# One decoder layer on one core: the same steps in another order of the turn, with tables of their own for the first and the last 900 steps

## The reference

```python
KV = x @ V;  V = 0.25 * V @ (13*I - KV @ (15*I - KV @ (7*I - KV)))      # pinv, 6 times, 64x64, 16 heads
out = attn1 @ (pinv(attn2) @ (attn3 @ v));  x = x + out @ Wout + bout   # 64 landmarks = means of 8 tokens
x = x + (softmax(mask(Q @ K.T / 4)) @ V) @ Wo.T + bo                    # cross-attention to 64 tokens
sel = argmax(softmax(gelu(x_n[last] @ Wp1 + bp1) @ Wp2 + bp2))          # one expert of 8 for each batch
x = x + 0.3 * ((gelu(x_n @ W1[sel] + b1[sel]) @ W2[sel] + b2[sel]) @ Wo_f + bo_f)
```

## Time and profile before

| what | us |
|---|---|
| median of 3 runs | 1443.07 (1442.46 to 1445.51) |
| span of the profiled execution | 1444.1 |
| TensorE busy in it | 1406.6 (97%) |
| VectorE / ScalarE / GpSimd busy | 1028.2 / 666.8 / 569.6 |

### The profile page before, as it was taken

The page is one execution under the profiler, slowest core; times in us unless marked ns, Lnnn a source line. Parts: engine busy times, 40 slices in busy tenths (PEclk is TensorE's granted clock), DMA queues, the critical chain, the costliest instruction groups (busy, mean ns, idle before and its releaser), DMA issues.

```text
span 1444.1 us, 54637 instructions
## 1 busy us (share of the span) xinstructions
PE 1406.6 (97%) x24180; PEld 927.0 (64%) x24180; DVE 1028.2 (71%) x2162; ACT 666.8 (46%) x1202; POOL 569.6 (39%) x799
## 2 busy tenths in 40 slices
...
DMA packets 40540, 53.25 MB, mean 37 GB/s; under 512 B 9698, under 2 KB 30450, under 8 KB 40306
## 3 DMA queue, kind: packets, MB, share of 16 engines
...
...
## 4 chain that ended last, share of the span: by engine, by line
PE 92%; DVE 5%; issue 2%; POOL 1%; ACT 0%; DVEq 0%; POOLq 0%; ACTq 0%
PE bank L1226 44%; PE bank L1244 8%; PE bank L1476 7%; PE bank L1254 6%; PE bank L1463 5%; PE bank L1431 2%; PE bank L1372 2%; PE bank L1325 2%; PE bank L1304 2%; PE bank L1234 2%; PE bank L1444 2%; PE bank L1361 2%; PE bank L1339 1%; PE bank L1465 1%; PE bank L1422 1%
## 5 line engine op out<-in xcount | busy, mean ns | idle before, releaser
L686 POOL TENSOR_TENSOR b<-ut,eye 128x256 f32<-128x256 f32 x192 | 136.4, 730 | 349.7 <-DVE ut L1066 320.2
L1096 DVE TENSOR_REDUCE m<-bank 128x8 f32<-128x512 f32 x128 | 82.3, 682 | 69.3 <-PE bank L1431 69.3
L1226 PE MATMUL bank<-xnT_a,wqkv 128*128 128x512 f32 x256 | 123.9, 607 | 0.0
L1226 PE MATMUL bank<-xnT_c,w1e 128*128 128x512 f32 x256 | 119.8, 604 | 0.0
L1226 PE MATMUL bank<-w2e,hT 128*128 128x256 f32 x512 | 117.9, 384 | 0.9 <-ACT hT L911 0.9
L1122 DVE RECIPROCAL oT_x<-bank 128x256 f32<-128x256 f32 x64 | 107.5, 1723 | 15.1 <-PE bank L1476 15.0
L1122 DVE RECIPROCAL oT<-bank 128x256 f32<-128x256 f32 x64 | 111.9, 1750 | 3.3 <-PE bank L1476 3.3
L1226 PEld LDWEIGHTS bank<-w2e,hT 128*128 128x128 f32 x512 | 94.9, 190 | 16.1 <-issue 1.7
L845 ACT ACTIVATE az<-bank 128x320 f32<-128x320 f32 x192 | 69.3, 401 | 76.2 <-PE bank L1244 73.6
L864 ACT ACTIVATE pT_x<-bank,neg_bias 128x512 f32<-128x512 f32 x128 | 78.0, 689 | 51.2 <-PE bank L1465 51.2
L1057 DVE SCALAR_TENSOR_TENSOR wb<-bank,eye 128x256 f32<-128x256 f32 x192 | 72.9, 413 | 34.7 <-PE bank L1244 34.6
...
## 6 DMA issues: line engine op xcount, KB each, us to landing
x_in<-in_x SPq DMA_DIRECT2D x16, 512.0 KB, 3.6
w1e<-in_W SPq DMA_DIRECT2D x16, 512.0 KB, 3.6
w2e<-w2o SPq DMA_DIRECT2D x16, 512.0 KB, 3.6
...
hT<-in_W2T SPq DMA_DIRECT2D x2, 512.0 KB, 5.7
...
w2o<-hT SPq DMA_DIRECT2D x2, 512.0 KB
```

The lines of the kernel that those rows point to most:

```text
L686: return g.tensor_tensor(b7[:, q, :], ut[:, q, :], eye[28 if it else 7][:].unsqueeze(1) .broadcast_to([P, 4, LM]), ALU.subtract).then_inc( ...
L1096: return v.tensor_reduce(m[x][:, :, j, 2 * k:2 * k + 2], tile(i, ("s" + x, k), j)[:].rearrange("p (t h c) -> p t h c", t=T, h=2), AX.X, AL ...
L1226: last = mm(dst, lhsT, rhs, start=(k == 0), stop=(k == len(pairs) - 1))
```

## The change

`TURN` is written anew: the same steps, at most 3 batches back instead of 6, in another order on every engine. A new table `FIRST` names the first 900 steps with their batch, as `LAST` does the last 900 (999 before). The setup steps stand in `FIRST` alone, so `once()` goes. The whole is 4411 steps before and after, 1307 of them on TensorE: before, 1011 came from the turns and 296 from `LAST`; now 264 from `FIRST`, 775 from the turns and 268 from `LAST`. `plan()`, `body()` and every instruction are as they were; lines after the tables lie 72 lower.

```diff
 TURN = """
-    S.fc D.mxx.1.3-5 D.mxx.0.1-5 D.mxx.0.3-5 P.y3.0-6 P.f.3-3 P.xnTa.0-3 A.xnTa.0-3 D.mxx.0.2-5
...
+    A.a.1-2 P.vx-3 D.recx.0.1-3 A.a.0-2 A.zT.1-2 D.recx.1.0-3 D.recx.1.1-3 P.z-2 G.b7.0.0-2 D.z-2 P.s1.1-2
...
+FIRST = """
+    S.x@0 S.w2.0@0 D.lnA@0 S.fc@0 G.lnA@0 P.f.0@0 S.w2.7@0 P.f.7@0 S.w2.6@0 D.nmA@0 P.f.6@0 P.xnTa.0@0
...
+    P.wx.0@15 A.nmC.1@15 P.y3.0@14 P.xnTc.1@15 D.wx.0@15 A.xnTc.1@15 P.gate@15 D.lnC.0@15 G.rsC.0@15
+    A.gate@15 P.logit@15 A.nmC.0@15 P.xnTc.0@15 A.xnTc.0@15 P.y3.1@14 D.logit@15 S.ew1@15 P.h.0@15 P.h.1@15
...
-def once(step):
-
-    return step[0] in ("fc", "w2", "f", "fb", "cn", "nmA", "cst", "kx")
...
 def program():
 
-    steps, last = [], set(LAST_STEPS)
+    steps, apart = [], set(FIRST_STEPS) | set(LAST_STEPS)
     for turn in range(BATCH + DEPTH):
         for engine, step, back in TURN_STEPS:
             i = turn - back
-            if 0 <= i < BATCH and not (i and once(step)):
-                if (engine, i, step) not in last:
-                    steps.append((engine, i, step))
-    return steps + LAST_STEPS
+            if 0 <= i < BATCH and (engine, i, step) not in apart:
+                steps.append((engine, i, step))
+    return FIRST_STEPS + steps + LAST_STEPS
```

More of the change, by code:

```diff
@@ new lines @@
+    D.rec1.0.1@15 D.o1.1@15 P.o1.0@15 P.xnTc.1@14 D.o1.0@15 P.w1.1@15 S.ctx@15 P.w1.0@15 D.w1.1@15
+    A.xnTc.1@14 G.rsC.0@14 D.lnB.1@15 D.w1.0@15 A.nmC.0@14 G.rsB@15 P.gate@14 D.lnB.0@15 G.lnB.0@15
+    P.y3.0@13 G.row@13 A.gate@14 A.nmB@15 P.xnTb.1@15 P.logit@14 A.xnTb.1@15 P.xnTb.0@15 P.xnTc.0@14
+    A.xnTb.0@15 P.qx.1@15 P.qx.0@15 A.qx.1@15 D.y3.0@13 P.sx.1@15 A.xnTc.0@14 A.qx.0@15 D.logit@14
+    D.mxx.1.0@15 D.mxx.1.3@15 P.sx.0@15 D.mxx.0.2@15 D.mxx.1.1@15 D.mxx.0.1@15 D.mxx.0.3@15 D.mxx.0.0@15
```

354 lines of the change are left out of this document (208 added, 146 removed).

## The result

The changed kernel takes 1447.87 us (median of 20 runs, 1441.85 to 1454.84), the kernel before 1443.64 (20 runs, 1440.89 to 1448.61). The ratio is 1.0029, 95% interval 1.0018 to 1.0040: slower, by little. The forecast was 1431, range 1417 to 1444. The profiled execution took 1447.92 with a span of 1446.1, 2.0 over the span of before. The new kernel's runs took 1.6 to 1.9 us more than their spans. Later runs of before took 1.8 to 2.1 over theirs, so its profiled execution (span 1444.1) took 1446 or little less, about 2 above its median. (Of the three runs that the prediction had, only 1445.51 is above that span; the text ahead of the prediction set the span beside the median and called it 1.0 above.) The new profile stands at its own median: the traces show half of the 4.2 us between the medians.

A forecast was written before the change was run, and what follows sets the result against it. The prediction took TensorE, busy 97% of the span, as the bound. From the span 1444.1: start −6.0, middle 0, neighbours −1.0, end −5.5 gives 1431.6; less 1.0 to the median 1430.6, rounded to 1431, range 1417 to 1444.

The forecast's parts named there:

- The end, −5.5: From 1240 us on: fewer idle waits in batches 14 and 15 win 5.5 us, bounds 0 to −9.
- the clock's place: From 1240 us on: the clock's cost of 5.6 us stays almost as it is, −0.1.
- The start, −6.0: 0 to 160 us: later first matmul +4.7, fewer waits −5.2, better clock −5.5, together −6.0 us.
- The lead: Before the first matmul: wfo queues behind other loads, first matmul at 10.4 us, costing +4.7 (+3.3 to +5.2).
- the clock: 95 to 160 us: of 6.3 us lost to the lower clock 0.8 stays, −5.5 (bounds 0 and −6.3).
- The middle, 0: The 9.5 turns: tight places cost 0.3 to 0.5 a turn against some 0.35 won; 0, bounds −2 and +14.
- the neighbours: Whole order: TensorE changes operand shape 725 times instead of 791; −1.0 us, from −7 to +6.
- The Trainium skill's rule: At 66 fewer shape changes, 190 ns a weight load: −12.5 instead of −1.0, giving 1419; rival, chance 0.03.
- The load of the expert: In each turn: w1e arrives with 1.1 us to spare, costed at nothing, bounds 0 and +9.5.
- The middle loses: Rival: in the turns, waits on wb or uz cost 1.5 us a turn, +14, giving 1445; chance 0.11.
- Everything pays: Rival: end's clock −3, middle's small waits −2, neighbours 5 more, giving 1421; chance 0.15.
- The order makes no difference: Rival: whole kernel, a stretch's gain turns into a wait somewhere else, giving 1443; chance 0.07.

The follow-up runs named there:

- e15: The changed kernel with two bank waits and a third wait reordered, the expert's bias on its own semaphore, and 15 spare matmuls in batch 15: 1444.56 us, ratio 1.0005.
- e16: The kernel before with 35 spare matmuls at the start alone, ahead of six steps that waited between 56 and 150 us: 1443.16 us, ratio 0.9993.
- e17: The kernel before with 45 spare matmuls, 27 at the start and 18 in batches 14 and 15 at the end: 1440.96 us, ratio 0.9978.
- e13: The changed kernel with its table of the last steps reordered at two places where TensorE waited for a bank: 1448.79 us, ratio 1.0030.
- e7: The changed kernel with its two tables cut to their first and last 600 steps, the turn filling what lay between: 1485.0 us, ratio 1.0289.
- e5: The changed kernel with 53 spare matmuls ahead of twelve TensorE steps that waited between 1137 and 1436 us: 1451.82 us, ratio 1.0059.
- e8: The changed kernel without its table of the last 900 steps, the turn going on to the end: 1469.09 us, ratio 1.0176.
- e9: The changed kernel with the expert's bias load on a semaphore of its own, for which TensorE does not wait: 1445.37 us, ratio 1.0018.
- e14: The changed kernel with two bank waits reordered, ScalarE's copy mTx@13 moved ahead of an exponential, and the expert's bias on its own semaphore: 1448.34 us, ratio 1.0032.
- e1: The first 450 steps in the new order, all others in the order of the kernel before: 1459.87 us, ratio 1.0116.
- e2: The first 700 steps in the new order, all others in the order of the kernel before: 1453.56 us, ratio 1.0068.
- e6: The kernel before with 95 spare matmuls ahead of 19 steps that waited at the start and the end: 1442.11 us, ratio 0.9991.
- e12: The changed kernel with v.0 (128x128) placed between sx.0 and sx.1 (32 rows) in the turn, two more shape changes a turn: 1454.66 us, one run.

## Why the prediction was wrong

**The end, −5.5: the step that failed most, with the wrong sign.** From 1120 us on the new order is 5.3 slower. The sum took the waits of before that would go, and added one that would come (+0.2). It did not price those that the new table brings: the bank waits (7.5 against 2.7 us), and a fall of the clock in the last batch's iteration 5. It even gave the clock's place a −0.1.

The failure has two places. Between 1120 and 1240 us, which the sum booked under the middle at nothing, the new order loses 3.9 us at a clock of 1.00, with 4.3 us of idle time where before has none; in every other trace that keeps the new table whole the lag rises by 2.9 us or more there. From 1240 us on the forecast −5.5 came out at +1.4 in the profile and at −0.6 to −1.5 in four other traces of the same table: idle time fell by 2.1 instead of 5.4, and what the clock takes differs from run to run. How much of the 5.3 is the clock stays open. Spare matmuls behind 1360 us were worth 3.8 in the medians and 2.5 in the traces in e15, but they were worth 2.2 in the old end too (e16 against e17), so the difference between the two ends is smaller than either.

That bank waits are where the rest goes is read from the trace alone and not shown: e13 took two of them away and gained nothing, as others opened behind the same row of VectorE's maxima. What would give that part back stays open.

**The start, −6.0: right in kind to 160 us and wrong to call it the start.** The lead (9.79 against 10.4) and the clock came about as worked out, and the lag at 160 us was 9.4 better, which is more than the −6.0. But 7.0 of it went between 160 and 340 us, in a stretch that the sum booked at nothing because before has no idle time there. A new order's fill ends where it ends, and here the profile has 6.8 us of idle time in that stretch. Whether another table would keep them busy stays open; e7 shows only that the turn would not. And e16 shows that the old order gets from the clock alone what remains, 2.4.

**The middle, 0: right in sum, by two terms that were both mis-sized.** Nine turns cost −0.8 against before in the profile. Of the kernels that left the new turn as it is, the lag between 340 and 1120 us changed by +0.4 (new), +5.1 (e5), +4.4 (e8), −0.5 (e9), +2.1 (e13), +1.4 (e14) and −2.1 (e15); of those with the old turn by +1.2 (before), +1.0, +0.4, −1.0, −0.8 and −1.0 (e1, e2, e6, e16, e17). The new turn's mean is 1.6 us above the old one's (1.5 against 0.0), by traces that differ by up to 7 us, so this is no more than a hint; that it varies more is plain. Compared step by step, some 2.7 us a turn were won at steps that stand behind their like (`h.1` 1.82 to 1.72, `tx.0` 1.29 to 1.18, `qx.0` 1.82 to 1.72) and 2.7 lost at tight places (`iZ.1` +0.27, `den1.0` +0.27, `jZ.0` +0.23, `w1.1` by the expert's load). The sum had −1.0 for the neighbours over the whole kernel and some 0.4 a turn for the waits. Its bounds held the total, though 2.7 a turn is far from either term. Two terms that cancel are luck as much as judgement.

The Trainium skill's rule that weight loads hide only behind matmuls of another row group (page "TensorE: Matmul & The Clock Gate", "What overlaps and what doesn't") would have given 0.19 us for each change of shape. e12 measured 0.1, and a price is there at all, which the forecast's −1.0 nearly denied.

**The load of the expert**, costed at nothing with 1.1 us to spare: `w1e` is in time, but TensorE also waits for the bias `b1e`, issued 0.6 us behind it, which the working left out. 0.17 us a turn (e9), within the bound given.

**The rivals.** "The middle loses" had the right side and the wrong place; it gave a turn 1.5 us more, and the turn got 0.15. "Everything pays" fell. None had the end as a loser. "The order makes no difference" (1443) had the right thing to say of the start, where the gain turned into waits behind it, and was given 0.07.
